# A two-layer decoder on one core: query features ahead of the numerators in a linear attention stage, and the last batch on banks of its own

## The reference, cut to what matters

```python
def _L1_xattn_ref(query, key, value, attention_mask, Wq, bq, Wk, bk, Wv, bv, Wqf, Wkf, Wo, bo):
    ...
    q_prime = jax.nn.relu(jnp.einsum('bhnd,fd->bhnf', q, Wqf))
    k_prime = jax.nn.relu(jnp.einsum('bhnd,fd->bhnf', k, Wkf))
    k_prime = k_prime * attention_mask[:, None, :, None]
    kv = jnp.einsum('bhnf,bhne->bhfe', k_prime, v)
    qkv = jnp.einsum('bhmf,bhfe->bhme', q_prime, kv)
    k_sum = jnp.sum(k_prime, axis=2)
    qk_sum = jnp.einsum('bhmf,bhf->bhm', q_prime, k_sum)[..., None]
    out = qkv / (qk_sum + 1e-08)
    out = out.transpose(0, 2, 1, 3).reshape(B, Sq, H)
    return out @ Wo.T + bo
```

## Time and profile before

| | |
|---|---|
| median of 3 runs | 972.36 us (971.62 to 973.23) |
| the profiled execution | 972.69 us, span 970.9 us |
| granted TensorE clock | 0.999 |
| busy in the span | PE 933.3, DVE 626.0, ACT 476.6, POOL 239.2 us |
| the linear attention loop | about 818 to 935 us of the span |

### The profile page before, as it was taken

The page is one execution under the profiler, slowest core; times in us unless marked ns, Lnnn a source line. Parts: engine busy times, 40 slices in busy tenths (PEclk is TensorE's granted clock), DMA queues, the critical chain, the costliest instruction groups (busy, mean ns, idle before and its releaser), DMA issues.

```text
span 970.9 us, 20007 instructions
## 1 busy us (share of the span) xinstructions
PE 933.3 (96%) x7633; PEld 793.2 (82%) x7633; DVE 626.0 (64%) x1385; ACT 476.6 (49%) x1594; POOL 239.2 (25%) x258
## 2 busy tenths in 40 slices
PE   7999999999999999999999999999999999999887
PEld 5777777799788888888888888888888887677667
DVE  5678887797875576564456464546455665777864
ACT  3887876544445454443444443444444554444431
POOL 2555787573011111111111011111102212110000
PEclk9999999999999999999999999999999999999999
DMA  7100000002340000000000000010002004000002
GB/s 283 60 2 2 2 2 2 2 1 90 95 166 1 1 1 2 1 1 2 1 1 1 2 1 1 20 42 2 1 22 68 1 1 176 2 2 1 3 1 87
DMA packets 10957, 27.89 MB, mean 29 GB/s; under 512 B 1840, under 2 KB 6992, under 8 KB 10224
## 3 DMA queue, kind: packets, MB, share of 16 engines
q1 hardware_dynamic: 10144, 26.41, 7.6%
q10 hardware_dynamic: 720, 0.20, 0.1%
HBM read 24.51 MB, written 2.10 MB: 27 GB/s over the span
## 4 chain that ended last, share of the span: by engine, by line
PE 84%; DVE 8%; ACT 4%; issue 2%; DMA 1%; POOL 0%; ACTq 0%; DVEq 0%
PE bank L50 15%; PE bank L52 14%; PE bank L51 14%; PE bank L2076 6%; PE bank L2025 5%; PE bank L395 3%; PE bank L405 3%; PE bank L2066 3%; PE bank L1940 2%; PE bank L1949 2%; PE bank L178 2%; PE bank L417 2%; PE bank L1552 1%; PE bank L1055 1%; PE bank L1066 1%
## 5 line engine op out<-in xcount | busy, mean ns | idle before, releaser
L1886 POOL TENSOR_TENSOR wa_prob<-wa_prob,wa_rsum 128x512 f32<-128x512 f32 x64 | 67.6, 1056 | 405.2 <-DVE wa_rsum L2459 405.2
L2258 ACT ACTIVATE wa_prob<-wa_prob,wa_negmax 128x128 f32<-128x128 f32 x256 | 99.8, 391 | 66.4 <-DVE wa_negmax L2448 66.1
L50 PE MATMUL bank<-norm_xT_hi,wide_hi 128*128 128x512 f32 x256 | 106.0, 414 | 0.2 <-DVE norm_xT_lo L189 0.2
L51 PE MATMUL bank<-norm_xT_lo,wide_hi 128*128 128x512 f32 x256 | 101.1, 395 | 0.0
L52 PE MATMUL bank<-norm_xT_hi,wide_lo 128*128 128x512 f32 x256 | 101.0, 395 | 0.0
L2515 DVE TENSOR_TENSOR wa_z_lo<-bank,wa_z_hi 128x512 fp32r<-128x512 f32 x64 | 44.3, 692 | 86.9 <-ACT wa_z_hi L2292 86.5
L587 ACT ACTIVATE v_prob<-bank,la_negmax 128x128 f32<-128x128 f32 x256 | 91.3, 400 | 1.1 <-DVE la_negmax L665 1.1
L2266 ACT COPY wa_q<-bank 128x512 f32<-128x512 f32 x64 | 37.6, 587 | 93.5 <-PE bank L52 93.5
L2273 ACT COPY wa_v<-bank 128x512 f32<-128x512 f32 x64 | 37.4, 585 | 89.5 <-PE bank L52 89.5
L332 POOL TENSOR_TENSOR v_prob<-v_prob,la_rsum 128x512 f32<-128x512 f32 x64 | 66.6, 1042 | 51.4 <-DVE la_rsum L670 51.3
L173 POOL TENSOR_TENSOR norm_rstd<-norm_rstd,minus_half 128x4 f32<-128x4 f32 x23 | 24.6, 1069 | 204.4 <-DVE norm_rstd L133 128.9
(11 more groups left out here) (272 smaller groups left out, 2374.1 us busy)
## 6 DMA issues: line engine op xcount, KB each, us to landing
wide_raw<-in_wide_w SPq DMA_DIRECT2D x16, 512.0 KB, 6.7
em_w<-in_em_w SPq DMA_DIRECT2D x1, 4096.0 KB, 13.5
lc_kt<-in_ctx_rev SPq DMA_DIRECT2D x1, 2048.0 KB, 10.6
lc_toep<-in_toeplitz SPq DMA_DIRECT2D x1, 2048.0 KB, 14.4
li_kt<-in_ctx_rev SPq DMA_DIRECT2D x4, 512.0 KB, 6.7
out_x<-x SPq DMA_DIRECT2D x8, 256.0 KB, 2.9
x<-in_x SPq DMA_DIRECT2D x3, 512.0 KB, 5.0
w_or_y<-in_l_w SPq DMA_DIRECT2D x1, 1024.0 KB, 5.7
```

What stands on the lines that cost most here:

```text
L50: nc.tensor.matmul(out, a[0], b[0], start=start, stop=False, skip_group_check=True)
L51: nc.tensor.matmul(out, a[0], b[1], start=False, stop=False, skip_group_check=True)
L1886: nc.gpsimd.tensor_tensor(prob[:, s], prob[:, s], rsum[:, s, :].unsqueeze(2).to_broadcast([P, G, P]), ALU.mult).then_inc(prob_ok, 1)
L2258: last = nc.scalar.activation(prob[:, s, j, :], prob[:, s, j, :], ACT.Exp, bias=negmax[:, s, j:j + 1], scale=SCALE, accum_out=sums[:, s, j ...
```

## The change

It has five parts. (1) In the batches with query features, TensorE issues them ahead of the numerators, and ScalarE keeps them ahead of the denominators. (2) In the third batch (batch 2) the keys of group 1 come before its queries, on TensorE and on ScalarE. (3) `VALUES_AHEAD` becomes true for batch 11. (4) The norm of part 2 of the mix is applied by ScalarE: VectorE writes minus the mean into a new `nbias`, GpSimd multiplies it by `rstd`, ScalarE computes x * rstd + nbias; the second half of its transposes directly follows the first, into a bank of its own (bank 5). (5) Batch 15 has its numerators in bank 1 and its denominators and their reciprocal in `qT`, which is no longer used by then; instead of the division of batch 14 it waits for the values of batch 15 to be kept.

```diff
@@ -146,6 +146,8 @@
             last = nc.vector.bn_aggr(self.meanvar[:, j, :], self.stats[:, j, :])
         last.then_inc(self.s_chain, 1)
         dve.wait_ge(self.s_chain, 2 * (self.base + it) + 2)
+        if negmean is not None:
+            nc.vector.tensor_scalar(negmean[:], self.meanvar[:, :, 0], -1.0, None, ALU.mult)
         nc.vector.tensor_scalar(self.rstd[:], self.meanvar[:, :, 1], EPS, None, ALU.add).then_inc(self.s_var, 1)
 
     def vector_apply_half(self, dve, it, g, half):
...
@@ -901,9 +903,9 @@
     SIM_AT = 3 * G + 1
     MIX_STATS = {2 * G - 1: (0, 0), 2 * G: (0, 1), 2 * G + 2: (1, 0), 2 * G + 3: (1, 1), 3 * G: (2, 0),
                  3 * G + 1: (2, 1)}
-    MIX_APPLY = {2 * G + 1: 0, 3 * G - 1: 1, 3 * G + 1: 2}
+    MIX_APPLY = {2 * G + 1: 0, 3 * G - 1: 1}
     SETUP_AT, LENGTH_AT = 1, 5
-    VALUES_AHEAD = [n < NB - 2 and n % G < 3 for n in range(NB)]
+    VALUES_AHEAD = [n < NB - 2 and (n % G < 3 or n > 2 * G) for n in range(NB)]
 
     def wait(eng, event, count):
         if count > 0:
...
@@ -912,6 +914,15 @@
     def heads_done(eng, heads):
 
         eng.wait_ge(pr.wide_o_ps, BASE + (NG - 1) * H + heads)
+
+    def nd_bank(n):
+        return b_nd if n < NB - 1 else banks[1]
+
+    def den_of(n):
+        return den[:] if n < NB - 1 else qT[:, 0, 0:D]
+
+    def rden_of(n):
+        return rden[:] if n < NB - 1 else qT[:, 1, 0:D]
 
     def out_bank(n):
         return (b_kv if n < NB - 1 else banks[4])[:, 0:D]
...
@@ -963,6 +974,8 @@
                 mix.gpsimd_setup(pool)
         for n in range(1, 3):
             norm.pool_rstd(pool, NG + n)
+        pool.wait_ge(norm.s_pool, norm.done(NG + 2))
+        nc.gpsimd.tensor_tensor(mix.nbias[:], mix.nbias[:], norm.rstd[:], ALU.mult).then_inc(mix.nbias_ok.sem, 1)
 
     def keys(pe, t, m, bank):
         if m == 0:
...
@@ -1047,12 +1060,15 @@
             t, j = divmod(n, G)
             reached(pe, kv_ok, n + 1)
             reached(pe, qf_ok, DC * (t + 1))
-            wait(pe, o_ok, n)
+            if n < NB - 1:
+                wait(pe, o_ok, n)
+            else:
+                reached(pe, v_ok, NB)
             for part in range(2):
                 for m in range(DC):
                     for r in range(RG):
                         at = (part * DC + m) * P
-                        last = nc.tensor.matmul(b_nd[32 * r:32 * r + 32, at:at + P],
+                        last = nc.tensor.matmul(nd_bank(n)[32 * r:32 * r + 32, at:at + P],
                                                 kv[:, n % 2, RG * m + r, part].rearrange("p e d -> p (e d)"),
                                                 qp[:, t % 2, RG * m + r, j * P:(j + 1) * P], start=True, stop=True)
             last.then_inc(nd_ps.sem, 1)
...
@@ -1082,13 +1098,19 @@
                 queries(pe, t, 0, b_p)
             if t < NG and j == 2:
                 reached(pe, kT_ok, DC * t + (2 if g else 1))
-                queries(pe, t, 1, b_p)
+                if g:
+                    queries(pe, t, 1, b_p)
+                else:
+                    keys(pe, 1, 1, b_p)
             for part, at in MIX_AT.items():
                 if n == at:
                     reached(pe, mix.kept if part else qT_ok, DC * part if part else DC * NG)
                     if part == 2:
                         reached(pe, mix.sim_ok, 1)
                     turn_x(NG + part, 0)
+                    if part == 2:
+                        reached(pe, kf_ok, NB)
+                        norm.turn_chunk(pe, NG + part, 1, mix.LAST_BANK(1))
 
         def ahead(n):
             g, j = divmod(n, G)
...
@@ -1112,10 +1134,10 @@
                 reached(pe, qT_ok, DC * t + 1)
                 keys(pe, t, 1 if g else 0, b_p)
             if n == 2:
-                reached(pe, qT_ok, DC * t + 2)
-                keys(pe, 1, 1, b_p)
+                reached(pe, kT_ok, DC * t + 2)
+                queries(pe, 1, 1, b_p)
             for part, at in MIX_AT.items():
-                if n == at:
+                if n == at and part < 2:
                     reached(pe, mix.kept, DC * part + 1)
                     turn_x(NG + part, 1)
 
...
@@ -1140,11 +1162,11 @@
             ahead(n)
             if 0 < n < NB - 1:
                 project(n - 1)
+            if t < NG and j >= 2:
+                query_features(t, j - 2)
             numerators_and_denominators(n)
             if n == NB - 1:
                 project(n - 1)
-            if t < NG and j >= 2:
-                query_features(t, j - 2)
             early(n)
             if n + 2 < NB and not VALUES_AHEAD[n]:
                 values(n + 2)
...
@@ -1211,8 +1233,10 @@
 
         def keep_den(n):
             reached(act, nd_ps, n + 1)
-            wait(act, o_ok, n)
-            nc.scalar.activation(den[:], b_nd[:, D:2 * D], ACT.Identity, bias=tiny[:, 0:1]).then_inc(den_ok.sem, 1)
+            if n < NB - 1:
+                wait(act, o_ok, n)
+            nc.scalar.activation(den_of(n), nd_bank(n)[:, D:2 * D], ACT.Identity, bias=tiny[:, 0:1])\
+                .then_inc(den_ok.sem, 1)
 
         keep_query_features(0, 0)
         keep_first_query_features()
...
@@ -1226,24 +1250,29 @@
                 norm.hi_chunk(act, t + 1, 0, b_p, norm.xT[0])
             if n == SIM_AT:
                 mix.scalar_sim(act, b_p)
-            keep_den(n)
             if t < NG and j >= 2:
                 keep_query_features(t, j - 2)
+            keep_den(n)
             if t < NG and j == 0 and g > 0:
                 keep_kT(act, t, 0, b_p)
             if t < NG and j in (1, 2):
-                keep_qT(act, t, j - 1, b_p)
+                if n == 2:
+                    keep_kT(act, 1, 1, b_p)
+                else:
+                    keep_qT(act, t, j - 1, b_p)
             for part, at in MIX_AT.items():
                 if n == at:
                     mix.scalar_keep(act, NG + part, part, 0)
             if n + 1 < NB:
                 keep_key_values(n + 1)
+            if n == MIX_AT[2] - 1:
+                mix.scalar_apply(act, NG + 2, 2)
+            if n == 2:
+                keep_qT(act, 1, 1, b_p)
             if t < NG and j == 0:
                 norm.hi_chunk(act, t, 1, b_p, norm.xT[0])
             if t < NG and j == 1:
                 keep_kT(act, t, 1 if g else 0, b_p)
-            if n == 2:
-                keep_kT(act, 1, 1, b_p)
             for part, at in MIX_AT.items():
                 if n == at:
                     mix.scalar_keep(act, NG + part, part, 1)
...
@@ -1293,8 +1322,8 @@
 
         def divide(n, chain):
             reached(dve, den_ok, n + 1)
-            chain.done(nc.vector.reciprocal(rden[:], den[:]))
-            nc.vector.tensor_tensor(o[:, n % 2].rearrange("p c t -> p (c t)"), b_nd[:, 0:D], rden[:], ALU.mult)\
+            chain.done(nc.vector.reciprocal(rden_of(n), den_of(n)))
+            nc.vector.tensor_tensor(o[:, n % 2].rearrange("p c t -> p (c t)"), nd_bank(n)[:, 0:D], rden_of(n), ALU.mult)\
                 .then_inc(o_ok.sem, 1)
 
         def update(n):
...
@@ -1631,12 +1661,26 @@
         reached(act, self.loaded, 16 * 3)
         self.nc.scalar.activation(self.sig[:], self.gates[:], ACT.Exp, scale=-1.0).then_inc(self.sig_in.sem, 1)
 
+    def LAST_BANK(self, c):
+        return self.pr.banks[(0, 5)[c]]
+
+    def scalar_apply(self, act, it, g):
+
+        norm = self.pr.norm
+        act.wait_ge(norm.s_tr, DC * norm.done(it - 1))
+        reached(act, self.nbias_ok, 1)
+        for j in range(G):
+            last = self.nc.scalar.activation(self.xn[:, j, :], self.pr.x[:, g * G + j, :], ACT.Identity,
+                                             bias=self.nbias[:, j:j + 1], scale=norm.rstd[:, j:j + 1])
+        last.then_inc(norm.s_xn, 1)
+
     def scalar_keep(self, act, it, g, c):
 
         norm = self.pr.norm
+        bank = self.LAST_BANK(c) if g == 2 else norm.banks[c]
         act.wait_ge(norm.s_tr, DC * (norm.done(it) - 1) + c + 1)
         for j in range(G):
-            last = self.nc.scalar.activation(self.xT[:, c, g * G + j, :], norm.banks[c][:, j * P:(j + 1) * P],
+            last = self.nc.scalar.activation(self.xT[:, c, g * G + j, :], bank[:, j * P:(j + 1) * P],
                                              ACT.Identity, accum_out=self.rep[:, c, g * G + j:g * G + j + 1])
         last.then_inc(self.kept.sem, 1)
 
```

7 lines of the change are left out of this document (4 added, 3 removed).

## The result

The changed kernel takes 977.75 us (976.64 to 980.01, six runs) against 972.43 of before on the same chip: a ratio of 1.0054, 95% interval 1.0045 to 1.0064. The direction was forecast, and the time lies above the forecast of 975.7 and 0.55 us above its range. The profiled execution took 977.99 us (span 976.2).

A forecast was written before the change was run, and what follows sets the result against it. TensorE's instruction stream was taken to bound the kernel. Terms −0.15 + 1.32 + 1.98 + 1.32 + 0.0 − 1.2 = +3.3 us against the median 972.36 gave 975.7 us (+0.34%), range 973.2 to 977.2.

The forecast's parts named there:

- the reciprocal 2.0 us later: Batches 2, 3, 6, 7, 10, 11: query features and their copies ahead of `li_den` start the reciprocal 2.16 us later.
- `norm_xn` in batch 7: Batch 6 to 7: the norm behind the late division delays TensorE's transposes, slack 0.2 us; +1.98 us.
- `li_va` in batches 4 and 8: Behind batches 3 and 7: `keep_values` after the late division delays the next values product; +1.32 us each.
- the late norm: Batches 2 to 3: transposes wait for the late `norm_xn`, so keys kept earlier gain almost nothing; together −0.15 us.
- keys first: Batch 2: keys of group 1 ahead of queries remove the wait for `li_kT`, 0.8 us gained.
- The tail: Last batches: batch 15's numerators, in bank 1, no longer wait for `li_o` of 14; −1.2 us, bounds −0.5 and −1.6.
- the price of a stall: All stall terms in the linear attention stage: each delay counted as idle time of TensorE, carried to the end.
- the term for the clock: Granted clock of TensorE behind the stalls: the forecast's sum has no amount for it.
- ScalarE's norm coming late: Rival, last batches: product and activations overrun their 0.2 us cover; at 1.4 late, 976.9 us; chance 0.10.
- GpSimd's product: Last batches: the added 128x4 product for the norm on ScalarE, taken at its upper bound of 1.01 us.
- the four activations with two per-partition operands: Last batches, ScalarE's norm: priced at 1.92 us by `li_den`, 2.06 by the skill page; hidden by 0.2 or nothing.

The follow-up runs named there:

- e6: Changed kernel, but ScalarE keeps denominators ahead of the query features again, TensorE's order staying as changed: 976.48 us, ratio 1.0037.
- e1: Changed kernel with numerators and denominators again ahead of query features on TensorE and ScalarE, `VALUES_AHEAD` as before: 970.79 us, ratio 0.9988.
- e8: Kernel before, with an added TensorE wait for `li_o` in batch 8 and five useless products ahead of that wait: 976.03 us, ratio 1.0032.
- e14: Changed kernel with query features ahead of numerators in batches 10 and 11 only, no useless products: 971.04 us, ratio 0.9982.
- e5: Changed kernel with three useless products in each of the three long TensorE waits of batches 4, 7 and 8: 975.16 us, ratio 1.0023.
- e2: Kernel before, plus only query features ahead of numerators and `VALUES_AHEAD` true for batch 11: 980.24 us, ratio 1.0086.
- e4: Changed kernel with three useless products in each wait for `li_va` of batches 4 and 8, batch 7's wait left open: 978.24 us, ratio 1.0066.
- e7: Kernel before, with an added idle TensorE wait for `li_o` behind the numerators of batch 8: 976.88 us, ratio 1.0046.
- e13: Changed kernel with query features first in batches 10 and 11 only, two useless products ahead of projections of batches 13 and 15: 970.05 us, ratio 0.9971.

## Why the prediction was right in direction and short in size

**Right: the mechanism and each of its terms.** The swap put the reciprocal 2.0 us later in its batch (forecast 2.16): 1.1 by TensorE's order and 0.9 by the copies ahead of `li_den`, by e6's trace. What was to be late next was late next: `norm_xn` in batch 7 (+1.91 for 1.98), `li_va` in batches 4 and 8 (+1.24 for 1.32), and in batch 2 to 3 the late norm took back what keys first gave (-0.13 for -0.15). The tail gave 1.15 for 1.2. The kernel with these waits filled took 975.16, where the forecast was 975.7. The terms were mostly a little large, 0.4 in the sum, in part because the reciprocal started 0.14 sooner behind the copies than I took.

**Wrong: the sum.** The step that failed is the price of a stall. Each was taken as the idle time of TensorE and nothing more; every duration behind a stall was copied from the trace of before, where the granted clock is 0.999, so that the term for the clock was nothing, and no reason was given for it. That trace had 6.7 us of waits in this stage, none longer than 1.7, and its profiled execution kept the clock. The change makes three more waits, 1.58, 1.86 and 1.58 long, and behind waits such as these TensorE is in part of the executions at 1.2 GHz for some 3.6 us; in the changed kernel's profile that cost 1.5 us behind the first of them (2.75 for the stretch, against 1.24 with the wait filled). No rival had this term either: the one above the forecast, ScalarE's norm coming late (976.9), did not occur.

**How far it goes.** The changed kernel's six executions have a mean granted clock of 0.993, 0.994 and four times 0.997; the traces of e1, e8 and e14 have 0.997 with one stretch of 3.6 us at the lower clock each, and e5 has 0.999 in eight of eleven. So at least one such stretch in each of the six fits, an estimate from the mean clocks, since only one of the six was profiled. The terms at full clock (+2.88) and one stretch (1.5) make +4.4 of the +5.3 in the median. The other 0.9 are not shown: the begin of the stage, which varies by 2 us between executions, is one candidate, a second stretch at the lower clock another.

**The small unknowns.** GpSimd's product took 0.20 us, where I took 1.01 as the upper bound, and the four activations with two per-partition operands 2.08, where I took 1.92:

```profile
923.65 0.20 POOL L978 TENSOR_TENSOR em_nbias<-em_nbias,norm_rstd 128x4 f32<-128x4 f32 x1
923.95 2.08 ACT L1673 ACTIVATE norm_xn<-x,em_nbias,norm_rstd 128x256 f32<-128x256 f32 x4 [0.49 <-POOL em_nbias L978]
```

They end at 926.03, and TensorE's transposes begin at 926.73: hidden by 0.7. The Trainium skill ("ScalarE: Activation LUTs", section "What ACT_TABLE_LOAD costs") gave 2.06 for them; the trace agrees, and it was a better price than the 1.92 from the neighbour's row, `li_den`. Neither changed the sum.

**What stays open.** What decides in which execution the clock falls behind a given wait. The waits of 1.57 to 1.86 us that the swap makes stand unfilled seven times in the traces of the changed kernel, e2 and e4, and two were followed by the lower clock. The wait for `li_o` of batch 13 (1.26 to 1.42 us), which the kernel before has as well, is in 15 of the 16 traces, and in six of them the lower clock stands behind it (e1, e4, e6, e7, e8, e14). These are counts from one execution of each kernel. Why the same kernel begins the stage up to 2 us sooner or later was not tried.

## What to carry to other kernels

A new wait of TensorE costs its length and, in part of the executions, a stretch at half the clock behind it: behind waits of 1.3 to 1.9 us this was 1.2 to 1.6 us each time it could be read (the changed kernel, e1, e4, e14), so a change that adds several such waits to a stream that was back to back is to be priced with a term for the clock, and one that removes them may gain more than their length. When VectorE or ScalarE works in order, ask of every instruction put ahead of another what stands behind that one in the queue: here a block of query features and its four copies ahead of one short activation delayed a norm with a slack of only 0.2 us and a values copy. Where a wait of TensorE can't be removed, products that nobody reads, shorter than the wait and in a free bank, held the clock there and brought 2.6 us by the medians where all three new waits were filled (e5; its trace shows 1.6 of them in the stage) and some 1 us, with overlapping intervals, in the last batches (e13); two of the three filled brought nothing (e4).
